# One matrix product for delta, B and C, with B and C spread over the partitions from DRAM

## The reference, cut to what matters

```python
xi = silu(conv1d(in_w @ x))                    # 96 channels, 1024 positions
dbl = einsum('bld,ed->ble', xi, xp_w)          # 6 + 16 + 16 values per position
dt, Bm, Cm = dbl[..., :6], dbl[..., 6:22], dbl[..., 22:]
delta = softplus(einsum('blr,dr->bld', dt, dt_w) + dt_b)
dA  = exp(delta[..., None] * A)                # 96 channels x 16 states
dBu = delta[..., None] * Bm[:, :, None, :] * xi[..., None]
h = dA_t * h + dBu_t                           # a scan over the 1024 positions
y = einsum('bds,bs->bd', h, C_t) + xi * Dp
out = out_w @ (y * silu(z))
```

## Time and profile before

| | |
|---|---|
| median of 3 runs | 4404.16 us (4399.27 to 4412.59) |
| the profiled execution's own time | 4406.85 us |
| its span | 4405.1 us |
| busy: TensorE, VectorE, ACT, GpSimd | 3987.6, 3400.8, 2901.3, 2380.0 us |
| mean granted TensorE clock | 0.938 |
| DMA, mean over the span | 131 GB/s |

### The profile page before, as it was taken

How to read it: one execution, slowest core, us unless ns; L and a number is a source line. 1 busy time by engine, 2 the same in 40 slices (tenths; PEclk the granted TensorE clock), 3 DMA queues, 4 the chain that set the end, 5 groups by cost and what they waited for, 6 DMA issues and landing times.

```text
span 4405.1 us, 42054 instructions
## 1 busy us (share of the span) xinstructions
PE 3987.6 (91%) x14264; PEld 1462.3 (33%) x14264; DVE 3400.8 (77%) x2997; ACT 2901.3 (66%) x3476; POOL 2380.0 (54%) x1108
## 2 busy tenths in 40 slices
PE   6889997999879998799987999889998899978997
PEld 2332234222342223422244222432234322342223
DVE  1469977799668996599965998669977699667996
ACT  1577747677577765767666775767757777476664
POOL 0137752577426874177732787228762477425773
PEclk9989999899899999899998999989989899898888
DMA  1147651667417763277624775257742576506671
GB/s 43 44 122 191 172 136 45 168 171 186 98 53 181 184 173 84 80 179 178 171 60 109 181 179 136 76 129 179 182 122 67 136 190 171 124 16 168 157 177 42
DMA packets 166830, 579.12 MB, mean 131 GB/s; under 512 B 22572, under 2 KB 23320, under 8 KB 163064
## 3 DMA queue, kind: packets, MB, share of 16 engines
q1 hardware_dynamic: 152280, 538.67, 48.8%
q10 hardware_dynamic: 14336, 37.76, 2.8%
HBM read 467.12 MB, written 71.48 MB: 122 GB/s over the span
## 4 chain that ended last, share of the span: by engine, by line
PE 65%; DVE 16%; ACT 10%; issue 5%; DMA 2%; POOL 0%; SPq 0%; DVEq 0%; POOLq 0%; ACTq 0%
PE ps L775 15%; PE ps L796 9%; PE ps L842 9%; DVE arena L1456 6%; PE ps L691 6%; PE ps L678 5%; DVE ps L1451 4%; PE ps L788 3%; PE ps L549 3%; PE ps L609 3%; PE ps L685 3%; PE ps L805 3%; ACT arena L940 2%; ACT arena L922 2%; PE ps L600 2%
## 5 line engine op out<-in xcount | busy, mean ns | idle before, releaser
L1538 POOL TENSOR_TENSOR arena<-arena 128x1024 f32<-128x1024 f32 x768 | 1803.0, 2357 | 890.5 <-DVE arena L1456 890.5
L1456 DVE TENSOR_TENSOR_SCAN arena<-arena,ps 128x1024 f32<-128x1024 f32 x768 | 1756.4, 2287 | 34.6 <-ACT arena L1145 8.3
L1451 DVE TENSOR_TENSOR ps<-ps,arena 128x1024 f32<-128x1024 f32 x768 | 933.0, 1215 | 220.8 <-PE ps L777 219.5
L1145 ACT ACTIVATE arena<-arena,a_all 128x1024 f32<-128x1024 f32 x768 | 865.8, 1141 | 318.5 <-DVE arena L1456 252.0
L775 PE MATMUL ps<-arena,spread 32*128 32x512 f32 x1536 | 909.7, 674 | 83.2 <-DVE arena L1456 83.2
L777 PE MATMUL ps<-arena,spread 32*128 32x512 f32 x1536 | 908.7, 674 | 0.0
L796 PE MATMUL ps<-arena,gather 128*32 128x512 f32 x3072 | 541.8, 652 | 4.5 <-POOL arena L1538 4.5
L842 PE MATMUL ps<-x 96*96 96x512 f32 x1008 | 505.6, 620 | 0.0
L775 PEld LDWEIGHTS ps<-arena,spread 32*128 32x128 f32 x1536 | 234.7, 190 | 727.4 <-issue 449.0
L1501 POOL TENSOR_TENSOR x<-x,arena 96x512 f32<-96x512 f32 x64 | 113.9, 1779 | 369.3 <-DVE arena L1321 369.3
L897 ACT ACT_TABLE_LOAD x226 | 290.0, 1283 | 24.9 <-DMA wo<-in_wo 20.9
(11 more groups left out here) (152 smaller groups left out, 5164.8 us busy)
## 6 DMA issues: line engine op xcount, KB each, us to landing
arena<-dl SPq DMA_DIRECT2D x768, 512.0 KB, 5.3
dl<-arena ACTq DMA_DIRECT2D x64, 384.0 KB, 5.8
x<-pn SPq DMA_DIRECT2D x56, 247.5 KB, 6.8
arena<-in_x SPq DMA_DIRECT2D x9, 1536.0 KB, 14.0
arena<-xq SPq DMA_DIRECT2D x64, 192.0 KB, 5.8
arena<-arena ACTq DMA_DIRECT2D x64, 192.0 KB, 5.0
out<-x SPq DMA_DIRECT2D x64, 192.0 KB, 2.1
arena<-xq SPq DMA_DIRECT2D x64, 191.8 KB, 5.1
```

Of the source, the lines that this page charges most:

```text
L1145: act.activation(da[:, m % DAS, :], dbc[:, m % DBC, :], ACT.Exp, scale=a_all[:, v // 2, m:m + 1]).then_inc(da_ready, 1)
L1451: dve.tensor_tensor(driven, driven, bmat[:, v % 2, :], ALU.mult).then_inc(bu_ready, 1)
L1456: dve.tensor_tensor_scan(hs[:, m % HSS, :], da[:, m % DAS, :], driven, 0.0, ALU.mult, ALU.add).then_inc(h_ready, 1)
L1538: pool.tensor_tensor(product, product, cmat[:, v % 2, :], ALU.mult).then_inc(pr_ready, 1)
```

## The change

Delta's weights (96 columns) and the 32 unrepeated columns of B and C stand side by side in `w_dbc`, so one product of 128 rows x 512 columns per half gives delta, B and C. The eight products with `xp_rep` and the eight copies per quadrant go (four of each per unit). After the softplus ACT copies the 32 rows of B and C (one instruction, 32 x 1024) and writes them to DRAM behind delta, both now in slot 4. SP spreads B and C of the next unit from DRAM over the 128 partitions, each row eight times, 512 KB each, in slots 8 and 9, and the convolution's window moves from slot 8 to slot 10. What waited for B or C to be copied (`b_ready`, `c_ready`) now waits for the transfers (`b_in`, `c_in`) or for the copy (`bc_ready`); the convolution's first tap waits for `bc_ready` where it waited for delta.

```diff
@@ -53,15 +53,16 @@
 PE_XI, PE_Z = 0, 2
-PE_DT, PE_B, PE_C, PE_OUT = 3, (5, 6), (7, 8), (9, 10)
-ACT_SILU, ACT_DL, ACT_U = 1, 6, 8
-ACT_DT, ACT_B, ACT_C, ACT_OUT = 4, (6, 7), (8, 9), (10, 11)
+PE_DBC, PE_OUT = 3, (9, 10)
+ACT_SILU, ACT_ROWS, ACT_U = 1, 4, 8
+ACT_DBC, ACT_OUT = 4, (10, 11)
 POOL_U = 5
 SP_SHIFT = 5
+SP_B, SP_C = 8, 9
 ACT_Y, POOL_GATE, S_SKIP, ACT_SILU_Z = 2, 1, 3, 3
 CONV_TAPS = {5: (0, 1), 6: (2, 3), 7: (4,), 8: (5, 6), 9: (7, 8)}
 ACT_GELU, PE_PW, ACT_PW, POOL_MIX = 10, 11, 0, 1
-SP_STORE, SP_LOAD = 3, 8
+SP_STORE, SP_LOAD = 3, 10
 LN_DEPTH = 2
@@ -107,8 +108,7 @@
         small_all = sb("small_all", [DI, QUADS, WS])
-        wdt_all = sb("wdt_all", [DI, QUADS, DI])
-        xp_rep = sb("xp_rep", [DI, QUADS, 2, 128])
+        w_dbc = sb("w_dbc", [DI, QUADS, DI + 2 * NS])
@@ -182,7 +182,8 @@
         cmat = two_of(cut(128, 2 * L))
-        delta = cut(DI, L)
+        delta_bc = cut(128, L)
+        delta, bc = delta_bc[0:DI], delta_bc[DI:128]
         u = two_of(cut(DI, 2 * L))
...
@@ -421,6 +422,24 @@
+                def spread_state(v, k, dst, landed, freed):
+                    V = p * UNITS + v
+                    sync.wait_ge(bc_out, (V + 1) * 16)
+                    if v >= 2:
+                        settled(sync)
+                        sync.wait_ge(freed, (V - 1) * G)
+                    rows = slice(DI + k * NS, DI + (k + 1) * NS)
+                    sync.dma_start(dst[:, v % 2, :],
+                                   a["dl"][v % 2][rows, :].rearrange("(n o) t -> n o t", o=1)
+                                   .broadcast_to([NS, DG, L])).then_inc(landed[v % 2], 16)
+                def spread_b(v):
+                    spread_state(v, 0, bmat, b_in, bu_ready)
+                def spread_c(v):
+                    spread_state(v, 1, cmat, c_in, pr_ready)
                 def load_window(t):
@@ -440,10 +459,17 @@
                         shifted(v + 1)
+                    if v and slot == SP_B:
+                        spread_b(v)
+                    if v and slot == SP_C:
+                        spread_c(v)
                 def first():
-                    for m in range(DBC):
-                        spread_delta(0, m)
+                    spread_delta(0, 0)
+                    spread_b(0)
+                    spread_delta(0, 1)
+                    spread_c(0)
+                    spread_delta(0, 2)
@@ -686,9 +712,9 @@
-                def of_xi(rows, bank, weights, i, c):
-                    return pe.matmul(ps[0:rows, bank, :], weights, xi[:, i, c * 512:(c + 1) * 512],
+                def of_xi(q, i, c):
+                    return pe.matmul(ps[:, 6 + c, :], w_dbc[:, q, :], xi[:, i, c * 512:(c + 1) * 512],
                                      start=True, stop=True)
@@ -699,21 +725,17 @@
                         pe.wait_ge(xi_ready, 2 * V + c + 1)
-                        of_xi(DI, 6 + c, wdt_all[:, 0, :], 0, c).then_inc(dt_ready, 1)
-                    for c in range(2):
-                        of_xi(128, 4 + c, xp_rep[:, 0, 0, :], 0, c).then_inc(b_ps, 1)
+                        of_xi(0, 0, c).then_inc(dt_ready, 1)
                     for c in range(2):
                         gate_in(0, 0, c, 2 + c)
                     pe.wait_ge(xs_in[1], (p * QUADS + 1) * XSL)
+                    pe.wait_ge(bc_ready, V + 1)
                     for c in range(2):
-                        pe.wait_ge(delta_ready, 2 * V + c + 1)
                         project_in(V + 1, 0, 1, c)
                 def first():
                     broadcast_u(0, 0)
-                    for c in range(2):
-                        of_xi(128, c, xp_rep[:, 0, 1, :], 0, c).then_inc(c_ps, 1)
@@ -726,7 +748,7 @@
                         pe.wait_ge(xs_in[i], (p * QUADS + q + 1) * XSL)
-                        pe.wait_ge(c_ready, 2 * V)
+                        pe.wait_ge(bc_ready, V)
                         if v >= 4 and i == 0:
@@ -738,24 +760,10 @@
                             gate_in(q, i, c, 6 + c)
-                    if slot == PE_DT:
+                    if slot == PE_DBC:
                         for c in range(2):
                             pe.wait_ge(sz_ready, 2 * V + c + 1)
-                            of_xi(DI, 6 + c, wdt_all[:, q, :], i, c).then_inc(dt_ready, 1)
-                    if slot in PE_B:
-                        c = PE_B.index(slot)
-                        if c == 0:
-                            pe.wait_ge(delta_ready, 2 * V + 1)
-                        else:
-                            pe.wait_ge(b_ready, 2 * V + 1)
-                        of_xi(128, 6, xp_rep[:, q, 0, :], i, c).then_inc(b_ps, 1)
-                    if slot in PE_C:
-                        c = PE_C.index(slot)
-                        if c == 0:
-                            pe.wait_ge(b_ready, 2 * V + 2)
-                        else:
-                            pe.wait_ge(c_ready, 2 * V + 1)
-                        of_xi(128, 6, xp_rep[:, q, 1, :], i, c).then_inc(c_ps, 1)
+                            of_xi(q, i, c).then_inc(dt_ready, 1)
...
@@ -835,7 +839,7 @@
                             if v + 1 < UNITS:
-                                pe.wait_ge(delta_ready, 2 * (p * UNITS + v + 2))
+                                pe.wait_ge(bc_ready, p * UNITS + v + 2)
                             else:
@@ -1062,27 +1066,25 @@
-                def keep_b(v, c, bank):
+                def keep_bc(v):
                     V = p * UNITS + v
-                    act.wait_ge(b_ps, 2 * V + c + 1)
-                    if v >= 2 and c == 0:
-                        act.wait_ge(bu_ready, (V - 1) * G)
-                    act.activation(part(bmat[:, v % 2, :], c), ps[:, bank, :], ACT.Copy).then_inc(b_ready, 1)
-                def keep_c(v, c, bank):
-                    V = p * UNITS + v
-                    act.wait_ge(c_ps, 2 * V + c + 1)
-                    if v >= 2 and c == 0:
-                        act.wait_ge(pr_ready, (V - 1) * G)
-                    act.activation(part(cmat[:, v % 2, :], c), ps[:, bank, :], ACT.Copy).then_inc(c_ready, 1)
+                    act.wait_ge(dt_ready, 2 * V + 2)
+                    if v:
+                        act.wait_ge(bc_out, V * 16)
+                    act.activation(bc, two(6)[DI:128], ACT.Copy).then_inc(bc_ready, 1)
                 def delta_to_rows(v):
                     V = p * UNITS + v
                     act.wait_ge(delta_ready, 2 * V + 2)
-                    act.dma_start(a["dl"][v % 2], delta).then_inc(delta_out, 16)
+                    act.dma_start(a["dl"][v % 2][0:DI], delta).then_inc(delta_out, 16)
+                def bc_to_rows(v):
+                    V = p * UNITS + v
+                    act.wait_ge(bc_ready, V + 1)
+                    act.dma_start(a["dl"][v % 2][DI:128], bc).then_inc(bc_out, 16)
@@ -1099,13 +1101,10 @@
                         exp_table()
-                    if slot == ACT_DT:
+                    if slot == ACT_DBC:
                         softplus(v)
                         exp_table()
-                    if slot in ACT_B:
-                        keep_b(v, ACT_B.index(slot), 6)
-                    if slot in ACT_C:
-                        keep_c(v, ACT_C.index(slot), 6)
+                        keep_bc(v)
@@ -1113,8 +1112,8 @@
                     delta_to_rows(0)
-                    for c in range(2):
-                        keep_b(0, c, 4 + c)
+                    keep_bc(0)
+                    bc_to_rows(0)
                     move_u(0)
@@ -1131,8 +1130,9 @@
                         exp_table()
-                    if slot == ACT_DL:
+                    if slot == ACT_ROWS:
                         delta_to_rows(v)
+                        bc_to_rows(v)
                     if slot == ACT_U:
@@ -1146,10 +1146,7 @@
                 def first():
-                    decay(0, 0)
-                    for c in range(2):
-                        keep_c(0, c, c)
-                    for m in range(1, DAS - 1):
+                    for m in range(DAS - 1):
                         decay(0, m)
@@ -1238,7 +1235,7 @@
             dve.wait_ge(setup_pe, 1)
-            dve.tensor_copy(wdt_all[:], ps[0:DI, 0:QUADS, 0:DI]).then_inc(setup_dve, 1)
+            dve.tensor_copy(w_dbc[:, :, 0:DI], ps[0:DI, 0:QUADS, 0:DI]).then_inc(setup_dve, 1)
             dve.wait_ge(setup_dve, 1)
@@ -1445,7 +1442,7 @@
                     if m == 0:
-                        dve.wait_ge(b_ready, 2 * V + 2)
+                        dve.wait_ge(b_in[v % 2], (p * QUADS + v // 2 + 1) * 16)
                     driven = two(2 + 2 * (m % 2))
...
@@ -1667,7 +1664,7 @@
     o["wo"] = wo
-    o["xp_rep"] = np.repeat(xp[:, rank:].reshape(QUADS, 2, NS, DI), DG, axis=2).transpose(3, 0, 1, 2)
+    o["xp_bc"] = xp[:, rank:].transpose(2, 0, 1)
     o["xp_dt"] = xp[:, 0:rank].transpose(1, 0, 2)
@@ -1687,7 +1684,7 @@
             for k, t in arrays.items()}
-    args["dl"] = nc.dram_tensor("dl", (2, DI, L), F32, kind="Internal").ap()
```

(1 more changed line is left out.)

18 lines of the change are left out of this document (7 added, 11 removed).

## The result

The changed kernel takes 4466.1 us (median; 4448.8 to 4476.6 in four runs) against 4406.8 us: a ratio of 1.0132, 95% interval 1.0094 to 1.0170. It is slower, by about 59 us; the forecast was 4379, with a range of 4322 to 4440.

The account below looks back on a forecast made before the run. TensorE was taken to bound the scan stage (88.0 us a two-unit cycle), VectorE right behind (82.66). Seven pairs winning 3.9 us each, the last 0, made 27 us off 4406.85: 4380, stated as 4379, range 4322 to 4440.

Parts of the forecast that it names:

- TensorE's products: Four B/C products of 0.86 us go per unit: 3.44 us of TensorE, 6.9 a cycle of two units.
- The wait for the copy of B and C: Slot 5's convolution waits for ACT's 1.02 us copy; TensorE idles there and at unit end; VectorE waits 1.75 us a cycle.
- The clock: TensorE's idling drops its clock once a cycle, costing 2.5 us (bounds 0 and 3.4); waits rise to 3.3 us a cycle.
- ACT and the transfers: B/C spreads delay step 2's delta spread to 8 to 9 us after issue; 0.5 us lost a cycle (bounds 0, 1.5 a unit).
- the 44.2: Unit time in us above which the prediction counts as wrong; so does a drop to 41.4.
- My own threshold, 8.8 us: A delta spread landing later than this after its issue would decide for (c): 8.6 plus ACT's 0.2.
- The rule on bandwidth: Skill's 341 GB/s would move a unit's 9.07 MB in 27 us; the prediction used the trace's 233 GB/s, 39 us.
- The start of a pair: First product waits for B's spread, queued second: 2.3 us lost a pair (bounds 0 and 4.5); unit 0 later wins 1.2.
- The sum: 3.9 us won in each of seven pairs, 27 us; last pair 0; 4406.85 becomes 4380, stated as 4379.
- (c): Rival: slower, late spreads for steps 1 to 3 delay ACT's chain; 4423 to 4464, put at 4435; chance 0.22.
- (b): Rival: the gain is lost again to dearer clock falls at both idle places; 4385 to 4415, put at 4402; chance 0.18.
- (a): Rival: the clock holds and spreads come in time; waits of 1.75 us a cycle, 4330; chance 0.20.

Follow-up runs that it names:

- mended version: Experiment 8: changed kernel with four delta buffers, bias copy before the decay, repeated pointwise product in slot 11, B/C copy before table load; 4315.4 us, 0.9801.
- experiment 1: Changed kernel with ScalarE's bias copy moved ahead of step 2's decay in slot 0; ratio 1.0116 to the kernel before.
- experiment 4: Changed kernel with four landing buffers for delta's spreads instead of three, each spread issued a step earlier; ratio 0.9970 to the kernel before.
- experiment 7: Changed kernel with four landing buffers, TensorE repeating its pointwise product in slot 11 of units 0, 1, 3, 5 and 7; ratio 1.0085.

## Why the prediction was wrong, step by step

- **TensorE's products: right.** I named 190 us less of busy time. The changed kernel shows 117, because its remaining products run longer at the lower clock; the mended version, at full clock in units 1 to 6, shows 189 (3987.6 to 3798.5), but with 35 products of 1.03 us added, 36 us; without them it would be 225, where 64 units x 3.44 make 220. The 190 that I named allowed for falls, so that 189 meets it is chance. Units that meet no wait take 41.4 us.
- **The wait for the copy of B and C: right in place.** The copy took 1.02 us, the number taken (row below). TensorE waited for it 38 times, 0.7 us each, in units 1 to 6. Where neither lateness nor a fall comes before, with four buffers, the idle places have the sizes worked out: 1.38 us in slot 5 of units with output (1.3 named), 1.06 to 1.19 at the end of the odd units (1.1 named), and 1.42 of wait in slot 0 of the odd ones (1.35 named).
- **The clock: right in kind, too small.** With lateness removed (four buffers), units 1 to 6 hold 261.1 - 248.0 = 13.1 us of waits, 4.4 a cycle, where I had 3.3 for waits and falls together. 1.4 of them are slot 0 of the odd units, without a fall; so falls cost about 3.0 a cycle and not 1.5. The fall itself was taken too short: 2.5 us lost for one, while the half clock lasted 6.9 us in the stretch with four buffers and 17 in experiment 1; at half the clock half of it is lost, 3.5 to 8.5 us. That the lateness from one fall shortens the idling in slot 5, "so one fall a cycle", holds in experiment 4 (in units with output it idles 0.56 us in slot 5 behind a fall and 1.38 without); its reverse is experiment 7.
- **ACT and the transfers: the step that failed.** I counted 0.5 us a cycle, and let only the spread for step 2 be late. Units 1 to 6 hold 271.9 - 248.0 = 23.9 us of waits, 8.0 a cycle; less the 4.4 of experiment 4, lateness costs 3.6, seven times the 0.5. The mean unit is 45.3 us, above the 44.2 that I had named as a sign of being wrong. Of the 87 us between 4379 and 4466 this term makes 3.1 x 3 x 7 = 65 and the clock's 1.1 x 3 x 7 = 23, an estimate from profiled executions. The average was right, 9.07 MB in a unit; what I did not do was follow the queue. I had step 2's spread land after 8 to 9 us. In units 1 to 6 of the seven pairs all 42 land later than 8.8, with a median of 12.0, and those of steps 1 and 3 have medians of 10.6 and 10.0; no other spread there lands later than 8.8. In the 30 us from 1050 on, the engines move 241 GB/s and a spread lands up to 12.9 us after its issue. The issues of SP (L433 is B, then C; L450 and L451 the window), the transfers, and the tile `dl`:

```profile
1053.48 2.59 SPq L421 DMA_DIRECT2D arena<-dl  x3
1056.46 0.51 SPq L433 DMA_DIRECT2D arena<-dl  x1
...
1064.06 16.78 SPq L421 DMA_DIRECT2D arena<-dl  x5
```

```profile
core 0 of [0], span 4447.0 us
...
DMA packets 2173, 7.23 MB, mean 241 GB/s; under 512 B 281, under 2 KB 281, under 8 KB 2171
```

```profile
ACT arena L1145: 11.7, 6
...
DMA to landing us min/median/max: 4.1/7.5/12.9
```

  (The last view says who waited for it, us and times.) From 1053.48 to 1064.06 SP issues eight spreads and the window, and ScalarE the move of half of u: 4.84 MB in 10.6 us, which at 241 GB/s take 20.1 us (an estimate from these rows). The last of them is step 2's, and lands 12.9 us after its issue. My own threshold, 8.8 us, held: 118 spreads of units 1 to 6 landed later, and 91 of their decays waited. I expected one spread near it, and three were beyond it. I had closed ACT's chain at the scans, and missed the copy of the bias behind the decay, by which a late decay stops TensorE, which then drops its clock; the scans themselves wait no more than before (31.5 and 34.6 us).
- **The rule on bandwidth.** The Trainium skill, DMA: Bandwidth & Descriptors, section Bandwidth, has 341 GB/s for a 1 MB load. Its table was measured with transfers issued from GpSimd; these are of 512 KB, issued from SP, beside others. The busiest stretch shown, 886.50 to 893.40 with four buffers, has 259 GB/s with the engines fully taken; the trace does not agree for these spreads.
- **The start of a pair: right in place and size.** The decay starts 3.54 us before the scan, not 1.25: 2.3 us, as worked out, because the product waits for B's spread. The stretches between the scans of two pairs cost 3.2 us each, 0.9 more than that; the rest was not followed up. Unit 0 gains 2.3 us (48.2 to 45.9), where I had 1.2.

```profile
797.45 1.02 ACT L1075 ACTIVATE arena<-ps 32x1024 f32<-32x1024 f32 x1 [0.40 <-ACT arena L1066]
...
805.12 1.15 ACT L1145 ACTIVATE arena<-arena,a_all 128x1024 f32<-128x1024 f32 x1 [0.84 <-DMA arena<-dl]
```

```profile
807.39 1.23 DVE L1448 TENSOR_TENSOR ps<-ps,arena 128x1024 f32<-128x1024 f32 x1 [9.08 <-DMA arena<-dl]
808.66 2.29 DVE L1453 TENSOR_TENSOR_SCAN arena<-arena,ps 128x1024 f32<-128x1024 f32 x1
```

- **The sum.** 4406.85 less 27 is 4380, and 2.7 less is 4377, not 4379; this changes nothing.
- **The rivals.** (c) had the right direction and place, and its upper end, 4464 with 90.0 us for a cycle, is nearly what was measured, 4466 with 90.6; I had put it at 4435. Its chain is right up to the decay: behind it the scans do not wait, TensorE does. What it called the bound, the rate of the transfers, is not one, as experiment 8 moves more per us. With the lateness removed (experiment 4) 4388.5 is measured, near the forecast and inside (b)'s band. (a), a clock that holds and spreads in time, came out only in experiment 8, and at 4315 below its 4330, as there the tap in slot 5 also starts earlier.
- **What stays open.** In the changed kernel the loss of 3.6 us a cycle comes almost whole over TensorE: ahead of its scans VectorE idles 31.5 us, with four buffers 29.0. How it divides into TensorE's waits for the bias copy (30.9 us in units 1 to 6 of the seven pairs) and the falls behind them was not separated. SP's place in the order is no part of it: of the 128 spreads of B and C only one waited for the write, 0.9 us. Why the clock falls behind one idle stretch and not behind another of the same length is open. Some last units of a pair (52.0 us in two pairs of experiment 8) were not followed up.
